# Sixteen replicating transfers of the attention's tokens, issued in diagonal order over batches and head groups

## The reference, cut to what matters

```
kf, qf, vf = (heads_flat(k), heads_flat(q), heads_flat(v))
dprod = softmax(einsum('bhtd,bhsd->bhts', qf, kf) / scale)
attn = einsum('bhts,bhsd->bhtd', dprod, vf)
attn = fno_layer(attn, proj_w, proj_skip_w, proj_skip_b, (H, W))
```

## Time and profile before

| | us |
|---|---|
| median of 3 runs | 431.83 |
| lowest and highest run | 427.73, 433.3 |
| span of the profiled execution | 424.2 |
| DVE busy in it | 338.0 (80%) |
| PE busy in it | 349.7 (82%) |
| ACT, POOL busy in it | 229.5, 213.0 |

### The profile page before, as it was taken

The page is one execution under the profiler, slowest core; times in us unless marked ns, Lnnn a source line. Parts: engine busy times, 40 slices in busy tenths (PEclk is TensorE's granted clock), DMA queues, the critical chain, the costliest instruction groups (busy, mean ns, idle before and its releaser), DMA issues.

```text
span 424.2 us, 7190 instructions
## 1 busy us (share of the span) xinstructions
PE 349.7 (82%) x2415; PEld 273.7 (65%) x2415; DVE 338.0 (80%) x995; ACT 229.5 (54%) x511; POOL 213.0 (50%) x261
## 2 busy tenths in 40 slices
PE   0289979997794899998999778878888789999950
PEld 0289965974352899987988748634454446767950
DVE  2999762766896967469999686999999759899991
ACT  0498851801023388545655125767886789899000
POOL 1389960000002699399892107887886579900000
PEclk9999999999998699999999969899999999999995
DMA  8999998999805000089799880142232500000998
GB/s 215 249 291 319 288 284 191 220 218 379 339 0 199 2 0 2 2 100 116 91 174 119 100 99 2 46 156 100 101 103 107 192 2 0 2 0 0 276 287 234
DMA packets 62999, 59.42 MB, mean 140 GB/s; under 512 B 5792, under 2 KB 55376, under 8 KB 60912
## 3 DMA queue, kind: packets, MB, share of 16 engines
q1 hardware_dynamic: 43232, 50.24, 40.0%
q0 software_dynamic: 16512, 8.39, 16.2%
q10 hardware_dynamic: 3216, 0.30, 0.7%
HBM read 38.84 MB, written 16.94 MB: 131 GB/s over the span
## 4 chain that ended last, share of the span: by engine, by line
DVE 34%; PE 32%; POOL 12%; DMA 6%; issue 5%; SPq 4%; ACT 4%; DVEq 0%; POOLq 0%; ACTq 0%
PE PS L632 30%; POOL BIG L569 8%; DVE SML L1196 6%; DVE BIG L1337 5%; DVE BIG L1529 4%; DVE BIG L1546 3%; SPq L511 3%; DMA BIG<-in_x 3%; DVE BIG L1613 3%; POOL BIG L588 2%; DMA BIG<-BIG 2%; PE PS L636 2%; DMA BIG<-xn_rows 2%; DVE BIG L1429 1%; DVE BIG L1425 1%
## 5 line engine op out<-in xcount | busy, mean ns | idle before, releaser
L632 PE MATMUL PS<-CST,BIG 128*128 128x128 f32 (+6 forms) x994 | 123.0, 312 | 13.1 <-ACT BIG L1004 4.5
L632 PEld LDWEIGHTS PS<-CST,BIG 128*128 128x128 f32 (+1 forms) x994 | 110.2, 193 | 28.8 <-DVE BIG L1529 8.3
L582 POOL COPY BIG<-BIG 128x512 f32<-128x512 f32 x24 | 29.9, 1291 | 79.2 <-DMA BIG<-xn_rows 75.3
L632 PE MATMUL PS<-BIG 128*128 128x128 f32 (+2 forms) x450 | 53.8, 368 | 5.9 <-DVE BIG L1337 5.4
L1196 DVE BATCH_NORM_STATS2 SML<-BIG 128x6 f32<-128x128 f32 x256 | 53.5, 279 | 5.8 <-DMA BIG<-in_x 4.4
L636 PEld LDWEIGHTS PS<-CST,BIG 128*128 128x128 f32 (+1 forms) x326 | 41.6, 183 | 19.5 <-issue 12.4
L632 PEld LDWEIGHTS PS<-BIG 128*128 128x128 f32 (+2 forms) x450 | 40.6, 168 | 16.7 <-issue 8.7
L636 PE MATMUL PS<-CST,BIG 128*128 128x128 f32 (+1 forms) x326 | 49.0, 291 | 2.5 <-ACT SML L400 1.4
L632 PE MATMUL PS<-BIG,SML 128*128 128x256 f32 (+4 forms) x230 | 48.8, 415 | 0.0
L400 ACT ACTIVATE BIG<-PS 128x512 f32<-128x512 f32 (+3 forms) x59 | 32.2, 569 | 26.0 <-PE PS L632 21.0
L569 POOL TENSOR_SCALAR BIG<-BIG,SML 128x128 f32<-128x128 f32 x84 | 40.3, 498 | 9.0 <-DVE SML L1216 9.0
(11 more groups left out here) (218 smaller groups left out, 487.3 us busy)
## 6 DMA issues: line engine op xcount, KB each, us to landing
xn_rows<-BIG SPq DMA_DIRECT2D x8, 1024.0 KB, 9.4
BIG<-xn_rows SPq DMA_DIRECT2D x8, 1024.0 KB, 9.2
BIG<-in_x POOLq DMA_DIRECT2D x8, 1024.0 KB, 11.0
BIG<-rs_rows SPq DMA_DIRECT2D x8, 1024.0 KB, 4.7
out_x<-BIG SPq DMA_DIRECT2D x32, 256.0 KB, 3.6
BIG<-wy_rows SPq DMA_DIRECT2D x16, 192.0 KB, 5.8
BIG<-BIG SPq DMA_DIRECT2D x16, 192.0 KB, 8.0
BIG<-in_L_conv_mixer_w SPq DMA_DIRECT2D x2, 544.0 KB, 9.1
```

What stands on the lines that cost most here:

```text
L582: pool.tensor_copy(x_mix[:, g % MIX_RING], columns(g)).then_inc(S("x_mix_pool"), 1)
L632: return pe.matmul(o, l, rhs, start=start, stop=stop, **k)
```

## The change

The loops around the sixteen transfers of line 511 are turned. Before, b was the outer loop and n the inner: (b, n) = (0,0) (0,1) (0,2) (0,3) (1,0) ... (3,3). Now k is the outer loop, b the inner, and n = (b + k) % 4: (0,0) (1,1) (2,2) (3,3), then (0,1) (1,2) (2,3) (3,0), then (0,2) (1,3) (2,0) (3,1), then (0,3) (1,0) (2,1) (3,2). The transfers themselves, their sizes, their semaphores and what waits for them are as they were.

```diff
             sp.wait_ge(S("ts"), 3)
-            for b in range(NB):
-                for n in range(HG):
+            for k in range(HG):
+                for b in range(NB):
+                    n = (b + k) % HG
                     sp.dma_start(xrep[TB * n:TB * n + TB, b].rearrange("s w k h -> s (w k h)"),
                                  ts[TB * b:TB * b + TB].rearrange("t w k h -> t (w k h)")).then_inc(S("rep_x_01" if b < 2 else "rep_x_23"), 16)
```

## The result

The changed kernel takes 431.1 us in the median of 22 runs (426.56 to 435.94), the kernel before 428.75 us in the median of 22 runs beside it (423.97 to 437.25). Nearly every kernel here has some slower executions, with more time at the lower TensorE clock; the ratios leave these out, the medians hold all. Only the first of the three is clear of 1.

The account below looks back on a forecast made before the run. The copies' landing, bound by transfer rate, and DVE's reaction were taken to set this stage. Span 424.2 + 0.6 = 424.8 us, plus 7.6 us around it, gave 432.4 us; range 427.6 to 435.8 us.

Parts of the forecast that it names:

- Place and stake: Copies' landing and DVE's two waits, 0.31 and 3.90 us: on the ending chain, whole stake 4.21 us, 1.0% of the time.
- Rate unchanged: Sixteen copies: the new order brings no change of rate, windows between 82 and 96 us staying at 210 to 230 GB/s.
- The rival of faster copies: Sixteen copies: engines a few copies apart read both sides at once, result 427.6 to 431.5 us; chance 0.25.
- The first wait ends with the fourteenth landing: DVE's wait on `rep_x_01`: ended by the fourteenth landing at 96.1 us, not by the eighth.
- The term of 0.6 us: DVE's products after the second wait: they go on at some 99.6 us instead of 99.01, a loss of 0.6 us.
- suppose each position lands when it did: Copy landings: each queue position keeps its earlier landing time, the fourteenth at 96.1 us and the sixteenth at 98.92 us.
- The clock: Rival: TensorE's 2.7 us gap ahead of `prob` lowers its clock, some 3.4 us reach DVE, up to 435.8 us; chance 0.12.
- if the clock falls ahead of `attend(1)`: TensorE in the changed kernel's profile: a sign of being wrong; the granted clock was to stay 1.00 from 97 to 115 us.
- SP's 14 us for the sixteen issues: SP's issuing of the sixteen copies: still needs 14 us in the changed kernel, after 13.99 us before.
- by a steady 7.9 to 9.0 us: Transfer landings: they follow their issues by this time, said against the rival of no visible effect, chance 0.08.
- the forecast 4 to 5 us: DVE ahead of the first two products of line 1337: one long wait of this length, none ahead of the next six.
- 7.6 us around the span: Whole kernel: the median of 431.83 us lies 7.6 us above the profiled span of 424.2 us; the shift is carried over.

Follow-up runs that it names:

- the first of the three: First measurement of the changed kernel against the kernel before, 22 runs each: ratio 1.0065 (1.0033 to 1.0096).
- the wide copies: Kernel before with the same bytes in four copies of 128 partitions instead of sixteen of 32, part of the computation wrong: ratio 0.9885 (0.9828 to 0.9942).
- the alternation with every copy: Sixteen copies reordered (0,0) (2,2) (1,1) (3,3) and so on, so the source changes side with every copy; one execution timed, 437.5 us, no ratio.
- the old order with the late wait: Kernel before, but the first fourteen copies count for DVE's first wait and the last two for its second: ratios 0.9983 and 1.0037.
- the diagonal within pairs: Kernel before with all eight copies of batches 0 and 1 first in diagonal order, then those of 2 and 3 likewise: ratio 0.9962 (0.9910 to 1.0014).
- r1_after: The changed kernel measured and profiled once more against the kernel before, nothing else changed: ratio 1.0031 (0.9976 to 1.0086).
- two queues: Kernel before with the eight copies of batches 2 and 3 issued by POOL on its own queue: ratio 1.0074 (1.0035 to 1.0114).
- r3_gap_filled: Changed kernel with 24 Gram matmul instructions moved ahead of TensorE's wait for the probabilities: ratio 1.0016 (0.9970 to 1.0063).
- the version with the head transfers moved: Kernel before with the last four head transfers (head group 3) issued behind the copies, on their own semaphore: ratios 0.9860 and 0.9837.
- r1_before: The kernel before measured and profiled once more against itself, nothing changed: ratio 0.9975 (0.9915 to 1.0035).

## Why the prediction was right, and where its sizes were off

**Place and stake: right.** The stage is on the path, and its whole stake was put at 4.21 us (the wide copies, which have neither wait, measure 1.15%, some 5 us, with an interval of 0.6 to 1.7%).

**Rate unchanged: right.** 221 to 224 GB/s in the four profiles with the changed order, 218 and 221 in the kernel before. The row that decided it was that of the head transfers, which alternate their destinations already. The rival of faster copies is out for this order; even the alternation with every copy brings only 3 to 8%.

**The first wait ends with the fourteenth landing: right,** shown by the old order with the late wait, which has the changed kernel's distance, and by the diagonal within pairs, which has that of the kernel before.

**The term of 0.6 us: right in sign, too small.** It measures 1.3 us. The step was "suppose each position lands when it did", with both positions from one profile, and it missed what a landing in the rows is. The views let a transfer land when its semaphore has counted 16 for it and 16 for each one ahead of it in its group. In the middle of a group, parts of the next transfer that are done early can fill that count; the last transfer of a group has nothing behind it, and its landing is that of the slowest part: of the 128 counts of `rep_x_01` in the kernel before, the last comes 0.94 us behind the one before it. In the kernel before the landings follow each other by 0.8 to 1.1 us (the ninth, right behind the eighth, by 0.13), but the eighth comes 1.66 us and the sixteenth 1.84 us behind the one before it: they are the last of `rep_x_01` and of `rep_x_23`. The fourteenth was read in the middle of a group, 0.83 us behind the thirteenth. As the last of its group it comes 1.63 and 1.62 us behind it in the two profiles of the late wait, where nothing differs from the kernel before but which transfers count for which wait. These 0.8 us on top of 0.6 make 1.4, for the 1.3 measured. The spread from one profile to the next is of nearly the same size (the third product 32.67 us after the first head issue in the profile that was read, 32.09 and 32.20 in the two others of its kind), so one profile could not carry a difference of 0.6 us in any case. Why one or two parts of a transfer come so late stays open.

**The clock: the mechanism came, its price did not.** The gap was forecast at 2.7 us and measured at 3.98 us in `r1_after`, at 3.3 to 3.9 us with the late wait and in the alternating order, and at 2.85 us with two queues. In all five the clock fell within it, and it did not in the two profiles of the changed kernel in which the scores were late and TensorE had no gap. The fall is one of the prediction's own signs of being wrong ("if the clock falls ahead of `attend(1)`"), and in `r1_after` it came. I priced it at 3.4 us for 10 us at the lower level; it lasted 6.8 us (3.4 with two queues) and cost nothing. The sum's own remark, that below about 5 us at the lower level TensorE's slack covers it, was too cautious: 6.8 us are covered as well. The prediction also has TensorE through with the first half of `attend(0)` by 104.0 us; with a start at 103.0 us and the 1.92 us of the earlier trace rows it is 104.9, which changes nothing, since the second half waits for DVE until then anyway.

**SP's 14 us for the sixteen issues: wrong, without effect.** It needed 11.98, 11.64 and 11.66 us with the diagonal, against 13.99 and 13.86 us. SP's timeline in `r1_after`, to be read against the earlier trace rows:

```profile
76.70 11.64 SPq L512 DMA_DIRECT2D BIG<-BIG  x16
```

**Landings "by a steady 7.9 to 9.0 us" after their issues: wrong, without effect.** In the kernel before they took 7.3 to 8.9 us for the copies and 3.3 to 9.0 us for the head transfers. Nor did the wait have the forecast 4 to 5 us in any profile of the changed kernel: it was 0.33, 6.01 and 2.02 us, since it depends on when the scores come. As long as they come before the fourteenth landing, the loss does not.

**7.6 us around the span: wrong.** Every later run lists its own span, and a run's time is 1.8 us more than that (434.23 us for the span of 432.4). The profiled execution of before was simply one of the shorter ones, of about 426 us. That the absolute forecast of 432.4 us comes so near to 431.1 us is luck: its base, the median of three runs, was 3.1 us above the 428.75 us of 22 runs, and the shift of 0.6 us that it added was smaller than the 2.4 us between the two medians.

**Open.** Of the whole-kernel ratios of the changed kernel, 1.0065, 1.0031 and 0.9997, the last two agree with 1.3 us (1.0030); the interval of the first begins just above it, at 1.0033. So the first measurement holds some 1.5 us, or chance, that the local reading does not explain. The stretch of 13.7 us at 1.2 GHz near 180 us is in two of the three profiles of the changed kernel and in neither of the kernel before (nor in `r3_gap_filled`, which has the changed order too); with it the way from the attention's sum to the first Gelu takes 59.4 to 60.1 us, without it 54.3 to 55.4. It is also in one of two profiles of the version with the head transfers moved and in that with alternating sides, and in neither with the late wait. A shorter one of 3.4 us stands there in `r1_before`. Whether a shift of a microsecond or so upstream makes it more likely can't be told from so few profiles.

## What to carry to other kernels

Before reordering transfers in a full queue, count at which position the last member of each awaited group now stands: an order that spreads the groups makes the first group wait for nearly the whole, and work that lay between the two waits loses its cover. A landing read in the middle of a group is too early for the last of a group; add the longer step that the trace shows at a group's end. Where a queue is bound by its bytes, look first at what stands ahead of the needed transfers: here moving four transfers that are needed 25 us later won what sixteen rearranged ones could not. Look for a row in which the hoped-for pattern already runs; here the head transfers did, and they showed no gain.

## What the runs showed of the hardware

- Copies of 32 partitions move 213 to 230 GB/s with all DMA engines busy, from SBUF to SBUF (windows of 12 us) as from DRAM (221 GB/s for the head transfers), those over 128 partitions 419 to 421 GB/s. Neither the order of sides nor a second queue changed that by more than 8%. The Trainium skill (SBUF — State Buffer, door 1, the port swizzle) gives half of the ports for such a span, and this trace agrees.
- An order in which the source changes side every one or two copies shortens SP's issuing (from 13.8 to 14.3 us for sixteen to 11.2 to 12.0, and to 10.88 us with a change at every copy); the diagonal within pairs of batches, whose sources stay on one side for eight copies, takes 13.81 us. The diagonal's fourteenth copy landed no sooner for it.
- A semaphore that counts several transfers is full only with the slowest part of the last one: with the copies of a batch in a row, the last landing of a group came 1.6 to 2.5 us behind the one before it, the next within 0.15 us of that, and the others 0.8 to 1.3 us apart.
- TensorE's clock fell to 1.2 GHz within gaps of 2.85 to 3.98 us without work, for 6.8 us in four profiles and 3.4 us in one, and DVE's distance from the third product to the sum of the attention's parts stayed between 33.38 and 33.42 us.
